# Attention kernel with hand-written queues: the centred pieces of x split before they are stored, another order of the first query tiles, and masking and maxima of the scores in one VectorE instruction

## The reference

```
y  = layernorm(x)
q  = rope(y @ Wq)        k = rope(ctx @ Wk)        v = ctx @ Wv
s  = q @ k.T / sqrt(128)
s  = where(mask == 0, -1e9, s)
x  = x + (softmax(s) @ v) @ Wo
W  = scales * (nibbles(qweight) - nibbles(qzeros))
out = x + layernorm(x) @ W + bias
```

## Time and profile before

| | |
|---|---|
| median of 3 runs | 2415.59 us (2408.92 to 2416.83) |
| the profiled execution: time, span | 2418.64 us, 2416.8 us |
| PE busy | 2353.0 us, 97% of the span |
| PE weight loads | 1975.2 us, 82% |
| DVE busy | 1336.1 us, 55% |
| ACT busy | 1114.9 us, 46% |
| POOL busy | 1180.8 us, 49% |
| DMA | 346.65 MB, mean 143 GB/s |
| mean granted clock of TensorE | 0.991 of full speed |

### The profile page before, as it was taken

The page is one execution under the profiler, slowest core; times in us unless marked ns, Lnnn a source line. Parts: engine busy times, 40 slices in busy tenths (PEclk is TensorE's granted clock), DMA queues, the critical chain, the costliest instruction groups (busy, mean ns, idle before and its releaser), DMA issues.

```text
span 2416.8 us, 33647 instructions
## 1 busy us (share of the span) xinstructions
PE 2353.0 (97%) x11552; PEld 1975.2 (82%) x11552; DVE 1336.1 (55%) x1949; ACT 1114.9 (46%) x2515; POOL 1180.8 (49%) x926
## 2 busy tenths in 40 slices
PE   8999998999999999899999999989999999999999
PEld 6887877888888888688888888868887877878887
DVE  4762554666666666666666666637743233343532
ACT  3222123667676667666766667643332222322010
POOL 1410535555665665556665566555664344355110
PEclk9999999999999999999999999999999999999999
DMA  7676674333434335343343333368554454443111
GB/s 262 237 178 223 233 246 152 92 102 100 113 103 114 105 106 155 113 127 102 93 117 106 106 112 103 111 212 284 202 191 168 149 178 166 143 177 113 44 44 53
DMA packets 201241, 346.65 MB, mean 143 GB/s; under 512 B 17744, under 2 KB 126544, under 8 KB 201168
## 3 DMA queue, kind: packets, MB, share of 16 engines
q1 hardware_dynamic: 187088, 310.06, 41.0%
q10 hardware_dynamic: 13312, 33.56, 4.2%
q0 software_dynamic: 768, 2.10, 0.3%
HBM read 238.69 MB, written 106.97 MB: 143 GB/s over the span
## 4 chain that ended last, share of the span: by engine, by line
PE 81%; DVE 7%; DMA 5%; ACT 3%; POOL 3%; issue 1%; SPq 1%; ACTq 0%; DVEq 0%; POOLq 0%
PE ps L208 18%; PE ps L209 18%; PE ps L210 18%; PE ps L690 7%; PE ps L691 7%; PE ps L692 7%; PE ps L622 4%; DMA scores<-in_ctx 2%; DVE rows L1226 1%; DMA xc_scratch<-xring 1%; DMA wraw<-in_L_xattn_Wo 1%; DMA xring<-in_x_tiles 1%; POOL s_buf L1322 1%; ACT probs L864 1%; PE ps L714 1%
## 5 line engine op out<-in xcount | busy, mean ns | idle before, releaser
L208 PE MATMUL ps<-act_t,wq_t 128*128 128x512 f32 x1280 | 512.5, 400 | 20.8 <-DVE act_t L1076 10.9
L210 PE MATMUL ps<-act_t,wq_t 128*128 128x512 f32 x1280 | 501.8, 392 | 0.0
L209 PE MATMUL ps<-act_t,wq_t 128*128 128x512 f32 x1280 | 501.6, 392 | 0.0
L690 PE MATMUL ps<-b_parts,a_parts 128*128 128x512 f32 x896 | 353.1, 394 | 11.3 <-POOL b_parts L1395 5.1
L1322 POOL TENSOR_TENSOR rope_tmp<-rope_tmp 128x512 f32<-128x512 f32 x144 | 192.4, 1336 | 341.8 <-DVE rope_tmp L1013 341.7
L691 PE MATMUL ps<-b_parts,a_parts 128*128 128x512 f32 x896 | 350.1, 391 | 0.0
L692 PE MATMUL ps<-b_parts,a_parts 128*128 128x512 f32 x896 | 349.7, 390 | 0.0
L1171 DVE TENSOR_TENSOR a_parts<-xring,a_parts 128x1024 fp32r<-128x1024 f32 x112 | 147.8, 1320 | 349.7 <-ACT a_parts L889 349.7
L1395 POOL TENSOR_TENSOR b_parts<-wraw,b_parts 128x512 fp32r<-128x512 f32 x112 | 195.7, 1748 | 275.1 <-ACT b_parts L894 275.1
L889 ACT ACTIVATE a_parts<-xring 128x1024 fp32r<-128x1024 f32 x112 | 118.7, 1060 | 415.8 <-PE ps L692 407.8
L208 PEld LDWEIGHTS ps<-act_t,wq_t 128*128 128x128 f32 x1280 | 242.5, 189 | 69.7 <-DVE act_t L1076 11.4
(11 more groups left out here) (111 smaller groups left out, 4437.8 us busy)
## 6 DMA issues: line engine op xcount, KB each, us to landing
xring<-left_scratch SPq DMA_DIRECT2D x112, 512.0 KB, 3.5
left_scratch<-s_buf SPq DMA_DIRECT2D x64, 640.0 KB, 5.3
wraw<-in_L_xattn_Wq SPq DMA_DIRECT2D x64, 512.0 KB, 4.0
wraw<-in_L_xattn_Wo SPq DMA_DIRECT2D x64, 512.0 KB, 4.4
v_scratch<-kv_t ACTq DMA_DIRECT2D x32, 512.0 KB, 3.0
k_scratch<-kv_t ACTq DMA_DIRECT2D x32, 512.0 KB, 5.1
kv_t<-k_scratch SPq DMA_DIRECT2D x64, 256.0 KB, 5.1
kv_t<-v_scratch SPq DMA_DIRECT2D x64, 256.0 KB, 4.6
```

What stands on the lines that cost most here:

```text
L208: eng.matmul(dst, lh, rh, start=(k == first), stop=False)
L209: eng.matmul(dst, lh, rl, start=False, stop=False)
L210: mm = eng.matmul(dst, ll, rh, start=False, stop=(k == last))
L690: pe.matmul(dst, lh, rh, start=(begins and not onto), stop=False, skip_group_check=True)
```

## The change

It has four parts.

1. **Pieces.** After the mean is subtracted, a piece is split at once: ACT writes its hi part and DVE its rest into `probs_t`, a single buffer (free in stage 1), in the same slot, u = 3 to 10 (`split_piece`, `rest_of_piece`). SP stores both parts, 1 MB instead of 0.5 MB a piece. ACT's split of piece i waits until the store of piece i-1 has landed. In group 7 the parts are loaded ready for use, 16 DMAs of 0.5 MB instead of 8, and `piece_hi` and `piece_lo` are gone.
2. **First tiles.** The first four query tiles come in the order (0,0), (0,1), (1,0), (1,1), so that head 0's weights can be replaced after two tiles; their replacement is moved forward on ACT and POOL. In turn 0 both halves of the query tile stand before `turn`. ACT loads its table of exponentials earlier.
3. **Masking.** The mask becomes an added number (0 or -1e30) in a buffer, made by `set_mask`, four DVE instructions of 128 x 512 for each half of the batch. One instruction, `tensor_tensor_reduce`, computes -(scores + mask) and its row minimum; there are four of 128 x 256 in a turn. `exponents` takes scale -1. The score banks are released when the minimum is done (`max_done`) instead of the copy (`s_copied`).
4. POOL's eight fills of the score buffers are gone.

```diff
@@ load and store of pieces (SP)
                 else:
-                    sp.wait_ge(xc_stored, (i - 1) * 16)
+                    sp.wait_ge(piece_lo, i - 1)
                 sp.dma_start(x_pair[i % 2], x_pieces[i]).then_inc(x_in[i % 2], 16)
             def store_piece(i):
-                sp.wait_ge(x_centred, i + 1)
-                sp.dma_start(xc_dram[i], x_pair[i % 2]).then_inc(xc_stored, 16)
+                sp.wait_ge(piece_lo, i + 1)
+                sp.dma_start(xc_dram[i], probs_t[:, :, :, :].bitcast(F32)).then_inc(xc_stored, 16)
...
-                if 3 <= u < 11:
-                    store_piece(u - 3)
-                    if u - 1 < 8:
-                        load_piece(u - 1)
+                if 4 <= u < 12:
+                    if u - 2 < 8:
+                        load_piece(u - 2)
+                    store_piece(u - 4)
@@ loads in group 7 (SP)
                         for k in range(4):
-                            sp.dma_start(act_v[:, 1, 2 * k:2 * k + 2, c * CT:(c + 1) * CT].bitcast(F32),
-                                         xc_dram[4 * c + k]).then_inc(xc_in[4 * c + k], 16)
+                            for l in range(2):
+                                sp.dma_start(act_v[:, l, 2 * k:2 * k + 2, c * CT:(c + 1) * CT].bitcast(F32),
+                                             xc_dram[4 * c + k, :, l, :, :]).then_inc(xc_in[4 * c + k], 16)
@@ PE, group 7 and the first turn
                     if switch and u8 in (4, 6):
-                        pe.wait_ge(x_lo, TT + 2 * (u8 - 4) + 2)
+                        for k in range(2):
+                            pe.wait_ge(xc_in[2 * (u8 - 4) + k], 32)
...
-                    turn(G, u8, first=first and u8 == 0)
+                    if not (first and u8 == 0):
+                        turn(G, u8)
...
+                    if first and u8 == 0:
+                        turn(G, u8, first=True)
@@ ACT, slots 3 to 10
+            def split_piece(i):
+                act.wait_ge(x_centred, i + 1)
+                if i > 0:
+                    act.wait_ge(xc_stored, i * 16)
+                act.activation(probs_t[:, 0, :, :], x_pair[i % 2], ACT.Copy).then_inc(piece_hi, 1)
...
+                if 3 <= u < 11:
+                    split_piece(u - 3)
@@ DVE, slots 3 to 10
+            def rest_of_piece(i):
+                dve.wait_ge(piece_hi, i + 1)
+                dve.tensor_tensor(probs_t[:, 1, :, :], x_pair[i % 2], probs_t[:, 0, :, :].bitcast(F32),
+                                  ALU.subtract).then_inc(piece_lo, 1)
...
+                if 3 <= u < 11:
+                    rest_of_piece(u - 3)
@@ DVE, masking
+            def set_mask(b, half):
+                dve.tensor_scalar(mask_add[:, b, :], mask8[:, half, b, :], 0, MASKED, ALU.is_equal, ALU.mult).then_inc(mask_set, 1)
...
-                    dve.copy_predicated(score_v[:, b, j, :], mask8[:, half, b, :], ps[:, BK_S + j, :]).then_inc(s_copied, 1)
-                for j in range(2):
-                    dve.wait_ge(s_copied, G * 16 + (2 * u8 + j + 1))
-                    dve.tensor_reduce(neg_max[:, par, j, :], score_v[:, b, j, :].rearrange("p (q k) -> p q k", q=2), AX.X,
-                                      ALU.max, negate=True).then_inc(max_done, 1)
+                    for qt in range(2):
+                        q = slice(qt * S, (qt + 1) * S)
+                        op = dve.tensor_tensor_reduce(score_v[:, par, j, q], ps[:, BK_S + j, q], mask_add[:, b, q], -1.0, 3e38,
+                                                      ALU.add, ALU.min, neg_max[:, par, j, qt:qt + 1])
+                    op.then_inc(max_done, 1)
@@ start of attention (ACT)
-            for m in range(3):
-                query_hi(0, 0, m, m)
+            act.wait_ge(ident_in, 16)
+            act.activation(row_sum[:, 0, 0, 0:1], identity[:, 0:1], ACT.Exp)
+            query_hi(0, FIRST_TILES[0], 0)
+            head_hi(0, 10 * 16, (q_done, 2))
+            query_hi(0, FIRST_TILES[1], 1)
+            query_hi(0, FIRST_TILES[2], 2)
             exponents(0, 0)
-            head_hi(0, 10 * 16, (q_done, 3))
             scaled(0, 0)
```

More of the change, by code:

```diff
@@ L126, in build @@
         mean_dram = dram("mean_scratch", [2, HALVES * HT])
[L127 removed]
+        xc_dram = dram("xc_scratch", [8, P, 2, 2, CT])
         rope_dram = dram("rope_scratch", [HALVES, 2, P, 2, CT])
@@ L586, in score @@
                 c = b // 2
-                if b % 2 == 0:
+                if first:
+                    pe.wait_ge(q_lo, 3)
+                elif b % 2 == 0:
                     pe.wait_ge(q_lo, G * UPG + (4 * par + 2 * c + 2))
@@ L851, in _, with query_hi @@
             store_unit(UNITS_A - 1)
-            def query_hi(G, par, i, m):
-                j, c = i % 2, i // 2
+            def query_hi(par, tile, m):
+                j, c = tile
                 act.wait_ge(q_sum, m + 1)
@@ L921, in attention @@
                         head_hi(0, G * 32 + (u8 // 4 * 16 + 11 * 16), (q_done, G * UPG + (u8 + 4)))
-                    if switch and u8 in (3, 4, 5, 6):
-                        piece_hi(2 * u8 - 5)
                     for kt in range(2):
@@ L928, in attention @@
                         act.activation(probs_t[:, kt, 0, :], ps[:, BK_T + kt, :], ACT.Copy).then_inc(pt_hi, 1)
-                    if switch and u8 in (2, 3, 4, 5):
-                        piece_hi(2 * u8 - 4)
                     if last and u8 in (5, 6):
@@ L1141, in _, with query_rot @@
                 tile_lo(t)
-            def query_rot(i, m, first=False):
-                j, c = i % 2, i // 2
+            def query_rot(bank, c, m, first=False):
                 dve.wait_ge(q_done, m + 1)
@@ L1153, in masked @@
                 if u8 < 4:
-                    dve.wait_ge(fill_done, half * 4 + b + 1)
+                    dve.wait_ge(mask_set, half * 4 + b + 1)
                 for j in range(2):
@@ L1185, in attention @@
                         masked(nG, nxt, nh)
-                    if switch and u8 in (3, 4, 5, 6):
-                        piece_lo(2 * u8 - 5)
                     if not (last and u8 == UPG - 1):
                         inverse_sum(nG, nxt)
+                    if switch and u8 >= 3 and u8 < 7:
+                        set_mask(u8 - 3, 1)
                     for kt in range(2):
@@ L1193, in attention @@
                                           ALU.subtract).then_inc(pt_lo, 1)
-                    if switch and u8 in (2, 3, 4, 5):
-                        piece_lo(2 * u8 - 4)
                     if last and u8 in (6, 7):
                         step_lo(u8 - 6)
+            dve.wait_ge(x_centred, 8)
+            for b in range(HB):
+                set_mask(b, 0)
             for c in range(2):
                 dve.wait_ge(rope_in[c], 16)
-            query_rot(0, 0, first=True)
-            query_rot(1, 1)
-            query_rot(2, 2)
+            for m in range(3):
+                query_rot(m % 2, FIRST_TILES[m][1], m, first=(m == 0))
             masked(0, 0, 0)
@@ L1363, in _, with query_lo @@
                 centre_tile(t)
-            def fill(b, half, wait=None):
-                if wait is not None:
-                    pool.wait_ge(*wait)
-                pool.memset(score_v[:, b, :, :], MASKED).then_inc(fill_done, 1)
-            def query_lo(par, i, m):
-                j, c = i % 2, i // 2
+            def query_lo(par, tile, m):
+                j, c = tile
                 pool.wait_ge(q_hi, m + 1)
@@ L1426, in attention @@
                         combine(G * 4 + 2, 0, (left_stored[1], G * 96 + 48))
-                    if switch and u8 >= 4:
-                        fill(b, 1, (exp_done, 2 * (60 + b) + 2))
                     if last and u8 in (2, 3):
@@ L1432, in attention @@
                         step_lo(u8 - 6)
-            pool.wait_ge(c_lo, C_WV0 + 4)
-            pool.wait_ge(tb_done, 8)
-            for b in range(HB):
-                fill(b, 0)
             for m in range(3):
                 rope_sum(rope_tmp, q_rot, m + 1, q_sum)
-                query_lo(0, m, m)
-            head_lo(0, 19)
+                query_lo(0, FIRST_TILES[m], m)
+                if m == 0:
+                    head_lo(0, 19)
             attention(0, first=True)
```

57 lines of the change are left out of this document (26 added, 31 removed).

## The result

The changed kernel took 2422.14 us in the median of 12 runs (2419.07 to 2426.56), the kernel before 2416.12 in 12 (2408.92 to 2418.89): 1.0030 times as long, 95% interval 1.0021 to 1.0038. That is +6.0 us, where 2426.0 (+10.4) was forecast, in a range from 2409 to 2436. The profiled span is 2424.8 us, before 2416.8.

What follows compares the result with a forecast made beforehand. PE was taken to bound attention, so gains lay only where it idles, and K_H1 would lose by a loop over each store. 28.8 - 16.9 - 1.5 = +10.4 us gave 2426 us, range 2409 to 2436.

Steps and rivals of the forecast that it cites:

- Part 1a: Switch in group 7: without the splits and rests, and with the doubled load in time, 16.9 us are gained.
- Part 1b: Pieces in K_H1: a loop over each store's landing takes 10.7 us a slot, so tiles and attention come 28.8 us later.
- lower bound of 22.2: K_H1: smallest forecast delay of tiles and attention in us, with the store's cycle at 9.6 us a slot.
- the only unmeasured length: K_H1: the landing of the store was called the only length not measured, as an argument for the stores landing sooner.
- rival A: K_H1: stores land sooner, the engines' chain sets slots of 6.8 and 9.2 us, shift 11.5 us, total 2409; chance 0.20.
- The fit of the Trainium skill: K_H1: 2.0 us plus bytes at 436 GB/s for a DMA; would shift the stage by 15 us, end about 2412.6.
- Part 2: Start of attention: the new order of first tiles removes the 5.27 us wait for weights; 1.5 us gained, between 0 and 3.
- Part 3: Masking in steady turns: four pairs take 2.4 us a turn instead of 2.8, worth nothing since hidden.
- The step's own sum: Masking: 1.9 us more a turn would be hidden, 4.5 us of masking in all.
- B: K_H1: PE's lead covers the stage and only the gains are left, -18.4 us, 2397; chance 0.06.
- C: Masking: the pass with the minimum is slow, PE waits in each turn, some +88 us, 2514; chance 0.05.
- D: Group 7: the doubled load comes late at 150 GB/s, giving back about 7 us, 2433; chance 0.07.

Runs made afterwards that it cites:

- e5: Changed kernel with the pieces stored unsplit in K_H1 and fetched, split and stored again during attention; median 15.7 us less than the kernel before.
- e4: Changed kernel with a second buffer for the split pieces, so a split needs only the last but one store landed; median +2.3 us on the kernel before.
- e6: e4 with the split ahead of `key_hi`, the rest behind the rotation, centring and stores a slot later; median -5.4 us on the kernel before.
- e3: Changed kernel with the first four query tiles, first turn and early copy of head 19 as before; median +7.1 us on the kernel before.
- e9: e5 with the first four query tiles, first turn and head 19 as before; 2399.36 us, against 2414.51 of the kernel before.
- e2: Kernel before with only the added mask and the accumulated minimum; 1.0005 times the kernel before, median +1.5 us.
- e7: Changed kernel with one unused reduction of 128 x 1024 bytes ahead of each score bank's passes; median +46.1 us on the kernel before.

## Why the prediction was right, and where its sizes were off

By the two distances the parts add up to 22.0 - 16.9 + 0.7 = +5.8 us, where 28.8 - 16.9 - 1.5 = +10.4 was forecast. The loss in K_H1 was put too high by 6.8 and the start of attention too low by 2.2. That the total is off by 4.6 only is in part luck.

**Part 1a, the switch: +16.9 regained, as worked out.** 22.87 - 5.98 in the changed kernel, and e5 shows it by itself.

**Part 1b, K_H1: right mechanism, mis-sized.** The cycle was worked out as 10.7 us a slot, all of them bound by the landing, which gave +28.8; +22.0 was measured, just under the lower bound of 22.2. PE's four waits for the weights came as said, 19.0 us in all instead of some 28. Term by term, from the end of a rest: issue of the load and the store's landing 0.4 + 5.9 + 2.0 = 8.3 forecast, 6.8 to 7.1 found. The view of the DMA issues has the eight stores at a median of 6.5 us:

```profile
xc_scratch<-probs_t SPq DMA_DIRECT2D x8, 1024.0 KB, 6.5
```

The six behind a load took 5.9 to 6.6 us, the last two, with no load ahead of them, 3.8 and 4.8. So doubling a store added less than 1 us to the 5.3 and 6.5 of 0.5 MB, where 2.0 was taken: this is the term that was mis-sized. The landing alone gives slots of 9.4. The odd slots are longer for a reason of which the prediction had no term: the centring, which now follows a later load, runs while `head_lo` runs. That makes the instruction 1.27 us longer and the slot, by the estimate above, 0.9. So "the only unmeasured length" was wrong: the engines' chain, of 9.2 us in an odd slot by rival A, was 10.3. From the first rest to the seventh the six slots took 58.7 us instead of 64.2, and the last 6.7 instead of 7.9; these are the 6.8 us. Without the collisions, which the forecast didn't have, K_H1 would have lost some 2.7 us less still, so one miss hid part of the other. By e4, 4.4 us of the 22 come back without the wait for the landing, 7.6 if its three new collisions are left out; e6 shows that the order of split, rest and centring in the slot costs 6.9 more. The fit of the Trainium skill ("DMA: Bandwidth & Descriptors", the anatomy of one DMA) put the landing of load and store 5.6 us behind the rest; 7.0 was measured. The section gives the fit for DMAs that GpSimd issues; these come from SP.

**Part 2, start of attention: -1.5 forecast, +0.7 found in the changed kernel.** Without part 2 (e3) it was +1.3, so the edit is worth 0.6 us at most, and in e5 and e9 it was 0.4 the other way. The wait for the head's weights went, as worked out. What failed is the sum from the second tile to the first scores, 5.4 + 2 + 5.4 + 5.4 = 18.2 us: it took 20.8 (413.46 to 434.25). Its last term, rotation, sum, hi and lo of the third tile, had nothing for POOL's `head_lo`, which the edit puts among them and which holds them up by 1.5 us. In the timelines:

```profile
413.46 0.79 PE L214 MATMUL ps<-act_t,wq_t 128*128 128x512 f32 x1 [5.11 <-DVE act_t L1087]
422.91 2.40 POOL L1398 TENSOR_TENSOR wq_t<-wraw,wq_t 128x1024 fp32r<-128x1024 f32 x1 [2.77 <-ACT wq_t L771]
425.27 1.28 POOL L1346 TENSOR_TENSOR rope_tmp<-rope_tmp 128x512 f32<-128x512 f32 x1
428.69 0.69 DVE L1029 TENSOR_TENSOR rope_tmp<-ps,rope 128x512 f32<-128x512 f32 x1 [4.88 <-POOL q_t L1393]
434.25 0.36 PE L214 MATMUL ps<-kv_t,q_t 128*128 128x256 f32 x1 [1.70 <-issue]
446.86 0.47 PE L214 MATMUL ps<-probs_t,kv_t 128*128 128x512 f32 x1 [1.12 <-DVE probs_t L1215]
```

PE waits 5.11 us for the tile's last rest. POOL's `head_lo`, now between the first tiles, keeps the second tile's rotation (ended at 423.81) from its sum until 425.27, the third tile's rotation waits behind that, and PE stands 1.70 us at the first scores and 1.12 at the first `weigh`.

**Part 3, masking: hidden, as said; its size 1.46 us instead of 2.4,** because the passes and the reads of the minimum overlap (0.35 us a pair instead of 0.42 + 0.18, and the read takes 0.08). e2 shows it alone, 1.0005. The slack was overstated. (The step's own sum, 2.8 + 1.9, is 4.7 and not 4.5, which changes nothing.) The row read, 1.9 us between a rest and its reader, is the slack of the rest. In the changed kernel, two turns of which each stands for a kind, with DVE's rests and PE's readers of the first (a pair of rests is 2 x 0.69):

```profile
1030.04 1.29 DVE L1215 TENSOR_TENSOR probs_t<-ps,probs_t 128x512 fp32r<-128x512 f32 x2 [1.25 <-ACT probs_t L943]
1039.90 1.29 DVE L1215 TENSOR_TENSOR probs_t<-ps,probs_t 128x512 fp32r<-128x512 f32 x2 [0.30 <-ACT probs_t L943]
...
1032.77 0.40 PE L214 MATMUL ps<-probs_t,kv_t 128*128 128x512 f32 x1
1041.92 0.40 PE L214 MATMUL ps<-probs_t,kv_t 128*128 128x512 f32 x1
```

The gaps are 2.0 and 1.3 us. Before, they were 1.9 and, in a turn of the other kind, 1.3:

```profile
1033.98 1.29 DVE L1192 TENSOR_TENSOR probs_t<-ps,probs_t 128x512 fp32r<-128x512 f32 x2 [0.30 <-ACT probs_t L928]
1035.94 0.40 PE L208 MATMUL ps<-probs_t,kv_t 128*128 128x512 f32 x1
```

With masking 1.1 us shorter both are as they were, so masking didn't set them, and the gap couldn't be added to the time of masking; and the turn that was read is not the kind with the least.

**The rivals.** A (the stores land sooner, the engines' chain sets the pace) was half of it: the landing came 1.3 us sooner, and the chain set every second slot, but at 10.3 us, not 9.2. Its sum, 2409, was therefore too low, as the forecast's was too high; the truth lay between them. B is refuted by the 19 us of waits; e5 gets most of its gain (-15.7 of -18.4), since there the split stands where PE has no wait. C fell with the 0.42 us of the pass, D with 40.00 us busy of 40.

**What stays open.** From the output stage's first product to the end it lasted 2.4 us longer in the profile of the changed kernel than before, and 2.4 us shorter in that of e6; no edit touches it, and I take it for the spread between runs. That POOL's instructions cause the longer ones of DVE is read from their ends in the traces; it wasn't tried to move the centring to another engine. Where half of e7's loss stands is open.

## What to carry to other kernels

Before you move work out of a stalled stretch, look for a place where the bounding engine has no wait: the same split cost 22 us in K_H1, where the engines hand each slot on without slack, and nothing that could be told in attention, where DVE was busy 54% of the time. When a buffer closes a loop over a store, a second buffer frees only the slots that the landing sets; what is next in the same loop is worth a look at the same time. And a gap between a producer and its reader in one row is the slack of that producer alone: to know how long another step may grow, lengthen it.

## What the runs showed of the hardware

- A DVE instruction with two inputs from SBUF doesn't run beside a two-input one of POOL. In nine traces, from 250 to 420 us, 58 were issued during a centring or a sum of POOL; every one of 128 x 1024 ended 1.07 to 1.09 us behind it, every one of 128 x 512 0.54 to 0.56. Issued at 310.14 beside a centring that ended at 311.56, `head_lo` took 2.50 us instead of 1.23; the rest of a key took 2.84 instead of 0.69 (e6). The rotations, which have one input from PSUM, kept 0.68 or 0.69 us from 250 to 365 us in seven traces, beside a centring too. The Trainium skill ("SBUF — State Buffer", Terms) says that DVE and GpSimd take turns on a shared port pair for a whole instruction, the other one blocked; the ends 1.08 and 0.55 us behind POOL's agree.
- The pass with the accumulated minimum over 128 x 256 takes 0.42 us and the read of the minimum 0.08, and the next pass starts 0.35 us after the one before, beside that read.
